# A vision block on one core: order of the passage from attention to the feed-forward part, and order of SP's transfers

## What is computed

```python
h = tok(x, W, b)                                    # shifted-patch embedding, then the cls token in front
h = h + attn(layernorm(h))                          # 4-bit fake quantisation of q, k, v, probabilities, output
#   out = fq(fq(softmax(fq(q) @ fq(k).T * scale)) @ fq(v)) @ fq(ww2).T + bb2
h = h + ffn(layernorm(h))
#   y = silu(gate) * up ; bitlinear(v, w, g) = quant(rmsnorm(v, g)) @ ternary(w).T, twice
```

## Time and profile before

| | |
|---|---|
| time, median of 3 runs (lowest to highest) | 1194.58 us (1193.99 to 1195.8) |
| the profiled execution: its time | 1195.78 us |
| the profiled execution: its span | 1194.0 us |
| around the span | 1.8 us |
| mean granted PE clock | 0.988 |
| PE / DVE / ACT / POOL busy, share of the span | 93% / 88% / 77% / 39% |

### The profile page before, as it was taken

How to read it: one execution, slowest core, us unless ns; L and a number is a source line. 1 busy time by engine, 2 the same in 40 slices (tenths; PEclk the granted TensorE clock), 3 DMA queues, 4 the chain that set the end, 5 groups by cost and what they waited for, 6 DMA issues and landing times.

```text
span 1194.0 us, 32030 instructions
## 1 busy us (share of the span) xinstructions
PE 1108.2 (93%) x11210; PEld 674.9 (57%) x11210; DVE 1056.6 (88%) x2028; ACT 923.6 (77%) x1832; POOL 466.1 (39%) x498
## 2 busy tenths in 40 slices
PE   7999999889999999999999999999867888888887
PEld 6999998445555555555555555555534444444444
DVE  7687666599999999999999999999887999999996
ACT  0000001889999999999999999999637999999997
POOL 5644344302211223221111232221236777766774
PEclk9999999999999999999999999999879999999999
DMA  8998998445655566556555655555532333333332
GB/s 292 313 314 249 316 306 236 137 138 150 152 150 150 131 147 156 145 150 150 145 150 147 141 150 151 149 151 143 146 98 64 105 101 101 103 99 99 99 95 71
DMA packets 157284, 187.87 MB, mean 157 GB/s; under 512 B 42864, under 2 KB 118464, under 8 KB 156928
## 3 DMA queue, kind: packets, MB, share of 16 engines
q1 hardware_dynamic: 115680, 156.92, 42.2%
q0 software_dynamic: 15936, 10.88, 9.4%
q10 hardware_dynamic: 25536, 18.31, 4.8%
HBM read 143.11 MB, written 36.12 MB: 150 GB/s over the span
## 4 chain that ended last, share of the span: by engine, by line
PE 73%; ACT 10%; issue 7%; DMA 3%; DVE 3%; POOL 2%; SPq 1%; ACTq 1%; DVEq 0%; POOLq 0%
PE psum L1139 14%; PE psum L1197 12%; PE psum L1260 12%; PE psum L1230 7%; PE psum L1200 7%; PE psum L1213 6%; PE psum L1247 6%; PE psum L1326 5%; ACT yi L674 3%; ACT zi L682 2%; ACT big L667 2%; PE psum L1306 1%; PE psum L1316 1%; DMA big<-xt 1%; POOL big L797 1%
## 5 line engine op out<-in xcount | busy, mean ns | idle before, releaser
L1075 DVE TENSOR_TENSOR pi<-big 128x2364 int16<-128x2364 f32 (+1 forms) x128 | 333.8, 2608 | 13.5 <-DMA big<-z_row 13.0
L769 POOL DMA_DIRECT2D h_res<-att x128 | 146.8, 1301 | 492.7 <-ACT att L601 484.0
L625 ACT ACTIVATE big<-psum 128x788 f32<-128x788 f32 (+1 forms) x384 | 330.3, 862 | 5.1 <-PE psum L1247 2.8
L587 ACT ACTIVATE qki<-psum 128x394 int16<-128x394 f32 x384 | 172.4, 508 | 25.5 <-PE psum L1200 13.8
L1139 PE MATMUL psum<-big 128*128 128x192 f32 (+1 forms) x1128 | 185.0, 327 | 2.3 <-DMA big<-xt 2.0
L1139 PEld LDWEIGHTS psum<-big 128*128 128x128 f32 (+1 forms) x1128 | 180.3, 188 | 5.5 <-DMA big<-xt 2.6
L1260 PE MATMUL psum<-big,sa_hot 128*32 128x197 f32 (+1 forms) x3072 | 168.2, 336 | 0.6 <-DVE zt L1099 0.6
L587 ACT ACT_TABLE_LOAD x1 | 1.3, 1283 | 189.5 <-PE psum L1200 189.5
L797 POOL TENSOR_TENSOR big<-big,goutb 128x512 f32<-128x512 f32 (+1 forms) x99 | 123.8, 1270 | 59.5 <-DVE big L1042 59.4
L1247 PE MATMUL psum<-qkb 64*128 64x197 bf16 (+1 forms) x1536 | 128.9, 246 | 1.3 <-DVE qkb L860 1.3
L596 ACT ACTIVATE vi<-psum 128x384 int16<-128x384 f32 (+1 forms) x256 | 115.7, 529 | 4.0 <-PE psum L1200 3.7
(11 more groups left out here) (109 smaller groups left out, 1812.6 us busy)
## 6 DMA issues: line engine op xcount, KB each, us to landing
big<-z_row SPq DMA_DIRECT2D x192, 394.0 KB, 5.0
big<-xt SPq DMA_DIRECT2D x98, 384.0 KB, 4.7
tin<-h_res SPq DMA_DIRECT2D x49, 192.0 KB, 3.0
tres<-h_res SPq DMA_DIRECT2D x49, 192.0 KB, 2.5
out<-oo SPq DMA_DIRECT2D x49, 192.0 KB, 2.6
h_res<-big ACTq DMA_DIRECT2D x84, 96.0 KB, 4.5
h_res<-att POOLq DMA_DIRECT2D x64, 96.0 KB, 3.4
x_int<-big ACTq DMA_DIRECT2D x84, 64.0 KB, 4.4
```

The lines of the kernel that those rows point to most:

```text
L587: act.activation(qki[:, k, :, :], psum[:, bank, 0:2 * N] .rearrange("p (c n) -> p c n", c=2), ACT.Copy, scale=factor[(F_Q, F_K)[b % 2]])\
L625: act.activation(ex[0:r, tri, t, 4 * g:4 * g + 4, :].rearrange("p (a h) n -> p a h n", a=2), psum[0:r, 2 * t:2 * t + 2, 0:2 * N] .rearrang ...
L769: pool.dma_start(h_res[bass.ds(b - 4, 1), t0:t0 + r, :].rearrange("a n d -> (a n) d"), att[0:r, par, t, :], accum_op=ALU.add).then_inc(s_a ...
L1075: v.tensor_tensor(pi[0:r, t, :, 0:N], ex[0:r, it, t, :, :], zb[0:r, ip, :, :], ALU.mult).then_inc(s_pi, 1)
```

## The change

It has four parts.

1. On SP, within a step of attention, `load_xT(b + 4)` stands behind the z chain instead of ahead of it.
2. In the passage, pair step 3 is cut up. On PE the inner products of tile pair 0 ("h"), then 4 filling matmuls on bank 4, then the turning of pair 1 ("x") stand ahead of image step B+2 (B = 64) instead of behind it; the 12 filling matmuls inside step B+2 go. On ACT the silu of pair 0 ("s") stands ahead of the quantising of pair 1 ("x"), both ahead of step B+2. On DVE the gated product of pair 0 ("g") stands ahead of the rest of pair step 3.
3. On POOL, pair step 3's product ("g") and pair step 3's and 4's roots ("x", "r") stand ahead of the additions of image 61 (step B+1). The additions of images 62 and 63, four transfers in one block ahead of pair step 6, are issued one in each of the pair steps 5 to 8, ahead of the product ("g").
4. `wait_added` asks for exactly the images that a tile pair needs up to t = 11 instead of t = 7.

```diff
--- before.py
+++ after.py
@@ -402,7 +402,7 @@
 
         def wait_added(eng, t):
 
-            last = (256 * (t + 1) - 1) // N if t < 8 else B - 1
+            last = (256 * (t + 1) - 1) // N if t < 12 else B - 1
             for p in range(2):
                 wait(eng, s_added[p], 32 * ((last - p) // 2 + 1))
 
@@ -471,10 +471,6 @@
                     for p in range(2):
                         sp.wait_ge(s_h1[p], stores_at(JOIN - 1 - (JOIN - 1 - p) % 2))
                         sp.wait_ge(s_x1[p], stores_at(LAST - (LAST - p) % 2))
-                if exists(b, 4):
-
-                    wait_apart(sp, full["v"], 4 * (b + 1))
-                    load_xT(b + 4)
                 if b == 0:
                     store_pack(JOIN)
                 if has_unit(b, -U1):
@@ -492,6 +488,10 @@
                         sp.dma_start(zb[:, 1 - par, 4 * g:4 * g + 4, :].rearrange("p h n -> p (h n)"),
                                      z_row[g, :, :].rearrange("h n -> (h n)").partition_broadcast(128))\
                           .then_inc(s_zb, 16)
+                if exists(b, 4):
+
+                    wait_apart(sp, full["v"], 4 * (b + 1))
+                    load_xT(b + 4)
                 if b == 1:
                     store_pack(LAST)
 
@@ -638,9 +638,11 @@
             act.wait_ge(s_stage_free, 4)
 
 
-            def pair_step(t, par, q):
+            def pair_step(t, par, q, parts="tsyxq"):
                 pair, oth = pair_of(t), 1 - par
-                if pair(2) == pair(5) == (128, 2):
+                if "t" not in parts:
+                    pass
+                elif pair(2) == pair(5) == (128, 2):
                     act.wait_ge(s_t["xT_summed"], t - 1)
                     act.wait_ge(s_t["yT_summed"], t - 4)
                     act.activation(zyT[:, par, :], turned.bitcast(i16)[:, 512:2048], ACT.Copy)\
@@ -658,7 +660,7 @@
                         act.activation(yT3[:, par, 0:n, :, 0:r], psum[:, 5, :].bitcast(i16)
                                        .rearrange("p (a c n) -> p a c n", a=2, c=4)[:, 0:n, :, 0:r], ACT.Copy)\
                            .then_inc(s_t["yT_read"], 1)
-                if at := pair(3):
+                if "s" in parts and (at := pair(3)):
                     r, n = at
                     for a in range(n):
                         act.wait_ge(s_t["hid"], 2 * (t - 3) + a + 1)
@@ -666,7 +668,7 @@
                         wait(act, s_t["y"], 2 * (t - 4) + a + 1)
                         act.activation(silu[0:r, a, :], psum[0:r, 2 * a + 1, :], ACT.Silu,
                                        scale=ft[0:r, (q + 2) % 4, 0, a:a + 1]).then_inc(s_t["silu"], 1)
-                if at := pair(4):
+                if "y" in parts and (at := pair(4)):
                     r, n = at
                     act.wait_ge(s_t["factors"], t)
                     wait(act, s_t["yT_summed"], t - 5)
@@ -674,7 +676,7 @@
                         ins = act.activation(yi3[0:r, par, a, :], yg[0:r, par, a, :], ACT.Copy,
                                              scale=pt[0:r, oth, S_, 1, a:a + 1])
                     ins.then_inc(s_t["yi"], 1)
-                if at := pair(1):
+                if "x" in parts and (at := pair(1)):
                     r, n = at
                     act.wait_ge(s_t["factors"], t)
                     wait(act, s_t["xT_summed"], t - 2)
@@ -682,7 +684,7 @@
                         ins = act.activation(zi3[0:r, oth, a, :], zc[0:r, oth, a, :], ACT.Copy,
                                              scale=pt[0:r, oth, S_, 0, a:a + 1])
                     ins.then_inc(s_t["xi"], 1)
-                if at := pair(3):
+                if "q" in parts and (at := pair(3)):
                     r, n = at
                     for a in range(n):
                         act.wait_ge(s_t["y"], 2 * (t - 3) + a + 1)
@@ -703,9 +705,12 @@
 
             images(image_step, -2, B + 1)
             act.activation(table[0:1, :], fac[0:1, 0:1], ACT.Silu)
-            pairs(pair_step, 0, 2)
+            pairs(pair_step, 0, 1)
+            pair_step(2, 0, 2, "t")
+            pair_step(3, 1, 3, "s")
+            pair_step(2, 0, 2, "x")
             images(image_step, B + 2, B + 2)
-            pairs(pair_step, 3, EARLY - 1)
+            pair_step(3, 1, 3, "txq")
             images(image_step, B + 3, B + 4)
             over_pairs(act, pair_step)
 
@@ -758,28 +763,32 @@
                     for s in range(PACK):
                         pool.dma_start(tile_rows(h_res, i, s), hp[:, i % 2, s, :]).then_inc(s_hlast, 16)
 
+            def add_attention(image, par, t):
+                t0, r = TOK[t]
+                wait_apart(pool, evac["y"], image + 1)
+                pool.dma_start(h_res[bass.ds(image, 1), t0:t0 + r, :].rearrange("a n d -> (a n) d"),
+                               att[0:r, par, t, :], accum_op=ALU.add).then_inc(s_added[par], 16)
+
             def image_step(b, par, tri):
                 if b == 4:
                     pool.wait_ge(s_hlast, 32 * PACK)
                     for p in range(2):
                         pool.wait_ge(s_h1[p], stores_at(JOIN - 1 - (JOIN - 1 - p) % 2))
                 if has_unit(b, -4 * U1):
-                    wait_apart(pool, evac["y"], b - 3)
-                    for t, (t0, r) in enumerate(TOK):
-                        pool.dma_start(h_res[bass.ds(b - 4, 1), t0:t0 + r, :].rearrange("a n d -> (a n) d"),
-                                       att[0:r, par, t, :], accum_op=ALU.add).then_inc(s_added[par], 16)
-
-
-
-            def pair_step(t, par, q):
+                    for t in range(2):
+                        add_attention(b - 4, par, t)
+
+
+
+            def pair_step(t, par, q, parts="rxg"):
                 pair, oth, g = pair_of(t), 1 - par, nc.gpsimd
-                if at := pair(4):
+                if "r" in parts and (at := pair(4)):
                     r, n = at
                     wait_apart(pool, s_t["square"], t - 3)
                     wait_apart(pool, s_t["factors"], t - 2)
                     g.tensor_tensor(val(1, par, RMS, r, n), val(1, par, T_, r, n), neg_half[0:r, 0:n], ALU.pow)\
                         .then_inc(s_t["y_rms"], 1)
-                if at := pair(0):
+                if "x" in parts and (at := pair(0)):
                     r, n = at
                     wait_apart(pool, s_t["mean_var"], t + 1)
                     wait_apart(pool, s_t["factors"], t - 1)
@@ -788,7 +797,7 @@
                     pool.wait_ge(s_t["vareps"], t + 1)
                     g.tensor_tensor(val(0, par, RMS, r, n), val(0, par, MS, r, n), neg_half[0:r, 0:n], ALU.pow)\
                         .then_inc(s_t["x_rms"], 1)
-                if at := pair(3):
+                if "g" in parts and (at := pair(3)):
                     r, n = at
                     for a in range(n):
                         pool.wait_ge(s_t["y"], 2 * (t - 3) + a + 1)
@@ -801,10 +810,16 @@
             pairs(pair_step, 0, 0)
             images(image_step, B, B)
             pairs(pair_step, 1, 2)
+            pair_step(3, 1, 3, "g")
+            pair_step(3, 1, 3, "x")
+            pair_step(4, 0, 0, "r")
             images(image_step, B + 1, B + 1)
-            pairs(pair_step, 3, 5)
-            images(image_step, B + 2, B + 3)
-            over_pairs(pool, pair_step, 6)
+            pair_step(4, 0, 0, "xg")
+            for t in range(5, 9):
+                pair_step(t, t % 2, t % 4, "rx")
+                add_attention(B - 2 + (t - 5) // 2, (t - 5) // 2, (t - 5) % 2)
+                pair_step(t, t % 2, t % 4, "g")
+            over_pairs(pool, pair_step, 9)
 
         @block.vector
         def _(dve):
@@ -958,10 +973,22 @@
                     v.memset(yy[:, :, HID:HID + 1], (HID * RMS_EPS) ** 0.5).then_inc(s_wdeq4, 1)
                     dve.wait_ge(s_wdeq4, 3)
 
-            def pair_step(t, par, q):
+            def pair_step(t, par, q, parts="mg"):
                 pair, oth = pair_of(t), 1 - par
                 V = lambda k: pt[:, oth, k, :, :]
                 step = s_t["step"]
+
+                def gated():
+
+                    if at := pair(3):
+                        rr, nn = at
+                        for a in range(nn):
+                            dve.wait_ge(s_t["silu"], 2 * (t - 3) + a + 1)
+                            wait(dve, s_t["yg"], 2 * (t - 4) + a + 1)
+                            if a == 0:
+                                wait(dve, s_t["square"], t - 3)
+                            v.scalar_tensor_tensor(yy[0:rr, a, 0:HID], psum[0:rr, 2 * a, :], ft[0:rr, (q + 2) % 4, 0, a:a + 1],
+                                                   silu[0:rr, a, :], ALU.mult, ALU.mult).then_inc(s_t["y"], 1)
 
                 def factors(phase):
                     x, y = pair(1), pair(4)
@@ -1000,6 +1027,9 @@
                         if a == n - 1:
                             ins.then_inc(s_t["zc"], 1)
 
+                if "m" not in parts:
+                    gated()
+                    return
```

(28 more changed lines are left out.)

## The result

The changed kernel takes 1353.24 us, median of 4 (1344.86 to 1359.75), against 1194.46 us, median of 4: ratio 1.132, 95% interval 1.126 to 1.139. The forecast was 1332 us, range 1282 to 1388.

The account below looks back on a forecast made before the run. PE was taken to set the pace in the attention stage, so its waits are paid in full. The terms 30 × (3.1 + 1.5) − 1 = +137 us gave 1332.8 on the profiled execution, a median of about 1332 us, range 1282 to 1388.

Parts of the forecast that it names:

- Which load slides: SP queue, attention: every load slides one place, about 10 us; image e+3, needed by PE's even step e, comes late.
- When it is issued: SP, attention: the load follows the spread at about T + 8.0, T being the start of y in PE's odd step.
- The floor of T + 4.03: SP, attention: earliest z store, 4.03 us after y starts in the odd step; DVE being early doesn't shorten it.
- How late: PE's query projection in even steps: image lands 3.1 us after its need at T + 11.07, range 2.4 to 4.0.
- How often: Attention stage: the stall comes once in two steps, pairs (4,5) to (62,63), 30 times.
- The clock: PE, attention: lower granted clock after each stall costs 1.5 us, bounds 0 and 3.4; 30 × 1.5 = 45 us.
- the row of 3.55 us: Passage, PE pause ahead of 916.87: about 3.4 us at the lower clock followed, losing 1.7 us of full-speed work.
- the clock holds: Rival, attention: stalls of 3.1 us but no change of clock level; +92, 1287 us; chance 0.12.
- low twice as long: Rival, attention: clock stays low twice as long, 3.4 us lost a stall; +194, 1389 us; chance 0.20.
- The passage: Parts 2 to 4: 2.7 us lost, 4.0 gained, net −1.3, called −1 us, range −5 to +3.
- the named wait: Passage: ACT's last `att` copy waits for image 61's additions, PE's pair step 4 for the copy: +2.7 us.
- The pause and the slow stretch ahead of pair steps 7 and 8: Passage, PE: spreading the additions removes the 3.55 us pause; 8.88 and 6.96 become 5.83 us, gain 4.2 less 0.2.

Follow-up runs that it names:

- the filled kernel: Kernel before with the SP move, plus 12 matmuls with unread results ahead of PE's wait for images in even steps: 1298.8 us, ratio 1.085.
- the passage alone: Changed kernel with the SP move undone, so parts 2 to 4 only: 1197.8 us, ratio 1.001 to the kernel before.
- the first experiments: Follow-up runs compared on the same chip with the kernel before, which had medians of 1195.9 to 1196.2 us there.
- the kernel with the load between: Kernel before with the load placed between the z store and the spread in all steps that have a z chain: 1196.6 us, ratio 1.002.
- the SP move alone: Kernel before with only the load moved behind the z chain on SP: 1348.5 us, ratio 1.130.

## Why the prediction held, step by step

- *Which load slides.* Right. The queue looks the same and serves the other image; the kernel with only the odd steps' loads in front runs at the old time, the one with all behind at 1348.5.
- *When it is issued.* T + 8.0 forecast, T + 8.05 in the instance shown and 7.99 to 8.55 over 28 pairs. The floor of T + 4.03 held in all of them, within 0.11 us.
- *How late.* 3.1 us forecast, 3.16 measured over 30 pauses, range 2.19 to 4.47 against 2.4 to 4.0.
- *How often.* 30 and 30.
- *The clock.* 1.5 us a stall forecast. In the trace it is 5.01 − 3.16 = 1.85 us. By the filled kernel, over medians, it is 1.66 us, to which the excess of its own lateness would have to be added. This is the term that was sized too low, 30 × 0.35 = 10 us, as the prediction said it would be first. I had taken a little off the row of 3.55 us because not each pause need trigger. That is so (two pauses of 2.2 to 2.3 us cost 0.15), but pauses of 3.7 and 4.5 us cost 3.75, more than the 1.7 of the row I leaned on. The average came out above that row. The rival "the clock holds" is refuted by the filled kernel; "low twice as long" is true of some stalls.
- *The passage.* One cost was left out, though the net is small. Pair step 4 came 2.95 us later against the last y but four, that of image 59 (46.39 against 43.44 us), where 2.7 was forecast, by the named wait. The pause and the slow stretch ahead of pair steps 7 and 8 went as said. But pair step 4 to 5 took 6.86 us against 4.84, so the gain behind the wait was 32.34 − 30.05 = 2.3 us for pair steps 4 to 9, not 4.0. The reason is the granted clock, 0.50 up to 1055, where the kernel before was back at 1.00 by 894. I had put the clock in pair step 4 at nothing, just after pricing 30 stalls with it. The new wait of 4.78 us isn't what lowered it: it was at 0.50 since 1036, and with that wait taken out pair step 4 to 5 still took 6.77 us. With part 2's order the clock falls in or right behind a shorter pause (1.6 to 3.2 us) ahead of the last y, in each of the traces looked at; which edit of part 2 moves it there wasn't tested. Net + 0.7 instead of − 1, and in the profile of the passage alone − 1.3; by its median the passage alone lies between − 0.4 and + 3.3 us.
- *Sum on the profiled execution.* 148.5 us before the passage (the y of image 59 is at 1002.35 and was at 853.88), 0.7 in it: 149.1. Forecast 137.
- *From the execution to the median.* The four executions span 15 us, and the profiled one was the lowest. So the median is 8 us above it, while I had set it 1 us below. That was luck in the drawing of one execution. I had read the scatter from the four executions of the kernel before, which span 2 us; its 19 on the chip of the first experiments span 10.5. Whether waits for landings widen the scatter further isn't shown.

## What to carry to other kernels

Before moving an instruction by one place in a queue that repeats, find out what stands beyond the end of the turn: behind the last item of a turn is the first of the next, so one place can be a whole turn. Then ask of each item for whom it is and when that is due, separately for the odd and the even turn. When a wait is put on the engine that sets the pace, price it twice, once for its length and once for the clock after it, and look at the clock ahead of it too; and where a change has several parts, measure each alone, for a good one (here the spread additions, 5.0 us) can be buried under the others.

## What the runs showed of the hardware beyond expectation

- Twelve matmuls that compute nothing, put into a wait that they can't shorten, made the kernel 50 us faster (1348.5 to 1298.8 us): the granted clock of the stage stayed at 0.99 instead of 0.90.
- A transposing load lands in 2.5 us (2.3 to 4.4, the kernel with the load between) with no spread of 394 KB right ahead of it, and in 5.7 us (4.5 to 7.6, the SP move alone) behind one; so a place 2.4 us sooner in the same step brought the landing forward by 5.6 us (T + 8.1 against a median of T + 13.7).
- Pauses of nearly the same length had very different prices (the two-step period less 20.14 us and less the next pause): 0.15 us after one of 2.31 us, 2.7 us after one of 2.35 us. The granted clock was 1.00 behind the first and 0.50 behind the second, up to about 345 us. The price is that of an average over 30, not that of a single row.
- An instruction of DVE on 128x4 values, median 0.16 us, took 2.13 us while POOL ran its product on 128x512, and ended within 0.03 us of it (0.85 us and 0.02 us in the passage alone). Other instructions of DVE ran beside such a product at their usual length, as the gated product and the statistics at 887 to 890 us in the passage alone.
